# A decoder layer in one kernel: in its cross-attention GpSimd adds a bias one step sooner, and ScalarE copies scores ahead of two context pieces

## The reference

```python
x = x + _L0_attn_ref(_layernorm(x), ...)
x = x + _L0_xattn_ref(_layernorm(x), ctx_1024, ctx_1024, ...)
x = x + _L0_ffn_ref(_layernorm(x), ...)      # last: y = real(ifft(fft(x) @ w)) + bias

def _L0_xattn_ref(query, key, value, Wq, bq, Wk, bk, Wv, bv, Wo, bo):     # 16 heads of 32, TOPK 32
    q, k, v = heads(query @ Wq.T + bq), heads(key @ Wk.T + bk), heads(value @ Wv.T + bv)
    scores = einsum('bhqd,bhkd->bhqk', q, k) / SCALE
    top_scores, top_idx = top_k(scores, 32)
    w = softmax(top_scores)
    out = einsum('bhqk,bhqkd->bhqd', w, take(v, top_idx))
    return merge(out) @ Wo.T + bo
```

## Time and profile before

| | |
|---|---|
| median of 3 runs | 2591.87 us (2591.48 to 2596.62) |
| profiled execution, its own time | 2596.9 us |
| span of the profile | 2595.1 us |
| busy: TensorE, VectorE | 2147.9 us (83%), 1987.7 us (77%) |
| busy: ScalarE, GpSimd | 1272.3 us (49%), 1275.2 us (49%) |
| mean granted clock of TensorE | 0.915 of full |

### The profile page before, as it was taken

How to read it: one execution, slowest core, us unless ns; L and a number is a source line. 1 busy time by engine, 2 the same in 40 slices (tenths; PEclk the granted TensorE clock), 3 DMA queues, 4 the chain that set the end, 5 groups by cost and what they waited for, 6 DMA issues and landing times. The chain is left out here.

```text
span 2595.1 us, 54503 instructions
## 1 busy us (share of the span) xinstructions
PE 2147.9 (83%) x19760; PEld 1691.8 (65%) x19760; DVE 1987.7 (77%) x3663; ACT 1272.3 (49%) x2464; POOL 1275.2 (49%) x1473
## 2 busy tenths in 40 slices
PE   2787878787885479898899888898899889898976
PEld 1555555555562367777777777777777777777764
DVE  4666665657542169998988989889889898898995
ACT  3232323232320257666666566566566566656653
POOL 2464545545442145555555454555455455545543
PEclk9899999999987789999999898899899889989997
DMA  5000000000004300100000000000000010001000
GB/s 170 8 20 10 19 9 19 9 19 9 16 8 145 92 18 16 30 19 20 25 25 16 20 23 26 20 19 24 27 16 19 20 30 19 20 16 34 6 8 10
DMA packets 41511, 70.29 MB, mean 27 GB/s; under 512 B 4638, under 2 KB 21166, under 8 KB 41260
## 3 DMA queue, kind: packets, MB, share of 16 engines
q1 hardware_dynamic: 35868, 56.31, 7.1%
q0 software_dynamic: 3632, 7.58, 1.2%
q10 hardware_dynamic: 1760, 3.28, 0.5%
HBM read 60.54 MB, written 9.86 MB: 27 GB/s over the span
## 5 line engine op out<-in xcount | busy, mean ns | idle before, releaser
L1346 DVE MATCH_REPLACE8 ca_W<-ca_top,ca_W 128x722 f32<-128x722 f32 (+1 forms) x624 | 554.0, 896 | 0.0
L1334 DVE MAX8 ca_top<-ca_W 128x8 f32<-128x722 f32 (+1 forms) x624 | 537.8, 900 | 1.2
L949 POOL TENSOR_TENSOR ca_S<-ca_S,ca_W 128x722 f32<-128x722 f32 (+1 forms) x208 | 357.2, 1737 | 262.3 <-ACT ca_W L1208 262.3
L88 PE MATMUL ca_pS<-ca_KH,ca_QH 128*128 128x362 f32 (+1 forms) x384 | 156.3, 407 | 139.2 <-ACT ca_S L1225 131.7
L926 POOL TENSOR_TENSOR ca_KL<-ca_K,ca_KH 128x384 fp32r<-128x384 f32 (+1 forms) x128 | 114.3, 893 | 310.8 <-ACT ca_KH L1200 308.4
L1324 DVE MAX8 ca_top<-ca_S 128x8 f32<-128x722 f32 (+1 forms) x208 | 180.8, 902 | 111.1 <-ACT ca_S L1225 96.3
L1230 ACT ACTIVATE ca_PT<-ca_pT 128x768 f32<-128x768 f32 (+1 forms) x208 | 164.0, 788 | 182.4 <-PE ca_pT L1081 181.5
L88 PE MATMUL ca_pF<-ca_cH,ca_WkH 128*128 128x338 f32 (+1 forms) x512 | 199.0, 389 | 23.3 <-POOL ca_cL L934 23.3
L1114 PE MATMUL ca_pO<-ca_PT,ca_V 128*32 128x56 f32 (+5 forms) x4608 | 217.3, 225 | 0.0
L364 POOL TENSOR_TENSOR sa_ss<-sa_ss,sa_minus_half 100x16 f32<-100x16 f32 x64 | 191.1, 2994 | 22.3 <-DVE sa_ss L534 22.2
L1208 ACT ACTIVATE ca_W<-ca_W,ca_shift 128x722 f32<-128x722 f32 (+1 forms) x208 | 185.8, 893 | 22.8 <-DVE ca_W L1346 22.8
(11 more groups left out here) (213 smaller groups left out, 5231.7 us busy)
## 6 DMA issues: line engine op xcount, KB each, us to landing
ca_raw<-in_ctxT SPq DMA_DIRECT2D x32, 384.0 KB, 3.4
ca_raw<-in_ctxT SPq DMA_DIRECT2D x32, 338.0 KB, 3.1
sa_xin<-in_x SPq DMA_DIRECT2D x16, 200.0 KB
sa_xres<-in_x SPq DMA_DIRECT2D x16, 200.0 KB
x_scratch<-sa_x SPq DMA_DIRECT2D x16, 200.0 KB
x_scratch<-y_scratch POOLq DMA_DIRECT2D x16, 200.0 KB, 13.0
ca_xin<-x_scratch SPq DMA_DIRECT2D x16, 200.0 KB
ca_x<-x_scratch SPq DMA_DIRECT2D x16, 200.0 KB
```

The source lines that it names most:

```text
L88: pe.matmul(out, ah, bh, start=start, stop=False)
L949: pool.tensor_tensor(S[k][rows, :], S[k][rows, :], W[r][rows, :], ALU.subtract).then_inc(p_ready, 1)
L1334: n_of[t.i] = order.mark(dve.max(top[r][rows, 8 * k:8 * k + 8], W[r][rows, :]))
L1346: ins = dve.match_replace(W[r][rows, :], eight, W[r][rows, :], REMOVED)
```

## The change

Two moves, nothing is removed or added. On GpSimd the addition of `bias_f` goes from the end of step 5 into step 4, behind `context_low`. On ScalarE `context_high` of the pieces 1 and 3 (steps 1 and 4) goes behind the copy of the first scores, the first projections' copies and the first output copy.

```diff
@@ GpSimd, body @@
                     if s in (1, 4) and nxt:
                         context_low(bn, 2 * (s // 3) + 1)
+                    if s == 4 and prev:
+                        pool.wait_ge(xn2_ready, b.count(1, 0))
+                        pool.tensor_tensor(x2[:, :], x2[:, :], bias_f[:, :], ALU.add).then_inc(x2f_ready, 1)
                     if s == 5 and nxt:
                         query_low(bn)
...
-                    if s == 5 and prev:
-                        pool.wait_ge(xn2_ready, b.count(1, 0))
-                        pool.tensor_tensor(x2[:, :], x2[:, :], bias_f[:, :], ALU.add).then_inc(x2f_ready, 1)
@@ ScalarE, body @@
                     for x in last:
                         exps_left(*x)
-                    if s in (1, 4) and nxt:
-                        context_high(bn, 2 * (s // 3) + 1)
...
                     if coming:
                         keep_scores(*coming[0])
...
                     if old:
                         keep_output(*old[0])
+                    if s in (1, 4) and nxt:
+                        context_high(bn, 2 * (s // 3) + 1)
```

## The result

The change makes the kernel slower: 2612.8 us median (2612.15 to 2613.93, 4 runs) against 2594.22 (2591.48 to 2596.62, 4 runs), a ratio of 1.0072 with a 95% interval of 1.0055 to 1.0090. Forecast were 2595 us and 2585 to 2606: the time lies outside the range, on the side of rival (c). The profiled execution took 2613.15 us, its span is 2611.3, 16.2 more than before.

The account below looks back on a forecast made before the run. The loop was taken to run over TensorE, ScalarE, GpSimd and the context load, with VectorE's 6 us slack. Terms -1.25 + 4 + 0.5 = +3.2 us on the median 2591.87 gave 2595 us, no tellable change; range 2585 to 2606.

Parts of the forecast that it names:

- rival (c): Steps 1 and 4: half clock falls wholly on the projections; up to 13 + 14 us slower, 2600 to 2618; chance 0.31.
- Part 1: GpSimd's bias add moved into its step 4 pause: free there, VectorE's wait cut to 2.7 us, gain only in last batch.
- The term of -1.25 us: Earlier bias add: gained once, in the last batch, which VectorE paces; bounds 0 and 20 or even 53 us.
- Part 2: Step 1: score copy ahead of cH, projections start 0.5 us earlier, pause moves behind the scores; +4 us in all.
- the same 4.6 us of half clock counted from the restart: Step 1: mean half clock stays 4.6 us but counts from the projections, ending them +0.4 a batch, +6 us.
- The other case: Step 1: the clock comes back at the same instants as now, so the earlier projections gain 0.27 us a batch, -4 us.
- the term of +4 us: Step 1 over 15 batches: +6 us and -4 us weighed 4 to 1; bounds -25 and +13 us.
- always the long stretch, +0.9, +13 us: Step 1's upper bound: every batch has the long half-clock stretch, +0.9 us a batch, +13 us.
- The weight of one in five for unchanged instants: Step 1: share given to the clock returning at the same instants (-4 us), in weighing 4 to 1.
- Part 3: Step 4: scores earlier, projections start unchanged, half clock 4.6 us from restart; +0.1 a batch, taken as +0.5 us in all.
- the whole 6.5 us on the projections: Step 4's upper bound: all the half clock lies on the projections, +0.9 us a batch, +14 us.
- Rival (b): Clock stays up in step 1 or 4, as the scores break the pause; 25 or 29 us faster, near 2565; chance 0.10.

Follow-up runs that it names:

- bias: Only the GpSimd move of the bias_f add, applied to the kernel before: 2592.69 us, ratio 0.9989 (0.9977 to 1.0001).
- act4: Only ScalarE's context_high move in step 4, applied to the kernel before: 2592.16 us, ratio 0.9998 (0.9988 to 1.0009).
- act1: Only ScalarE's context_high move in step 1, applied to the kernel before: 2606.61 us, ratio 1.0048 (1.0031 to 1.0066).
- act14: Only the two ScalarE moves, in steps 1 and 4, applied to the kernel before: 2611.04 us, ratio 1.0060 (1.0043 to 1.0078).
- fill_act1: act1 plus 22 unused TensorE matmuls ahead of the wait for cL in step 1 only: 2557.40 us, ratio to before 0.9857.
- fill_after: The changed kernel plus unused TensorE matmuls ahead of the wait for cL, 22 in step 1, 17 in step 4: 2533.95 us, ratio to before 0.9762.
- fill_half: The changed kernel plus half the unused matmuls, 11 in step 1 and 8 in step 4: 2541.17 us, ratio to before 0.9789.

## Why the prediction was wrong

**What bounds the kernel: right.** VectorE's 6 us a batch were slack. `bias` freed 44 us of them in 13 batches, and the program gained 1 to 3 us, if anything.

**Part 1: right in each step.** The add stands in GpSimd's pause, which fell from 5.13 to 3.89 us (3.8 forecast); VectorE waits 2.7 us for the product; 2.2 us of new waits stand ahead of the first scores. The add takes 1.27 us beside VectorE's replacement and maximum, as the row had it, and the replacement beside it takes 0.90 us. The Trainium skill's page SBUF — State Buffer, "SBUF: two separate sides", has VectorE instructions with two SBUF inputs and those of GpSimd block each other; no such delay shows here. Whether the replacement counts as one with two inputs, no run here tells. Not foreseen was the wait for `rstd`, 13.3 us, which costs nothing, as VectorE does not pace. The term of -1.25 us measured -1.3 to -2.8 in `bias`, not clear of zero. In the last batch, where the prediction put it, ScalarE's waits for VectorE's replacements fell from 21.7 to 20.3 us.

**Part 2, the step that failed: half clock counted from the restart of the matmuls.** The order came as forecast: the copy ahead of `cH`, `cH` not later, the projections 0.45 us earlier (0.5 forecast), the pause 4.2 us (4.5). The term was built on "the same 4.6 us of half clock counted from the restart". Measured were 5.18 us in the mean. Counted so, 8 of 15 batches had a short stretch before (2.9 to 3.9 us), and only 2 have one now (3.0 us). At 0.45 us lost per microsecond the 0.58 us more are 0.26 of the 0.5 us a batch by which the term was short. The rest is in the other numbers of the sum: the projections ended 7.3 us behind the old start of the scores, not 7.4. (The 0.64 that the prediction puts behind the gap of 4.35 us belongs to another batch; the batch of that gap has 0.65.) The other case, a clock that comes back at the same instants, did not come either: it comes back 2.3 us later behind `cH`. So the term of +4 us, with its bound "always the long stretch, +0.9, +13 us", was at this bound: +0.89 a batch, 13.4 us. The weight of one in five for unchanged instants was wrong too: only in those 2 batches (8.68 and 8.80 us) is N below the old mean of 8.84.

**Part 3: the same step, and the larger miss.** The term was +0.5 us, the trace of the changed kernel has 0.74 a batch, 11.1 us. The start of the projections was right. But the half clock was again taken as 4.6 us from the restart of the projections, where 4.4 had been. In the traces the stretch keeps its 6.8 us, begins 1.5 us later, and lies with 5.7 us on the projections, where 4.3 did: close to the bound "the whole 6.5 us on the projections". That `act4` costs nothing agrees with the term of 0.5, but by luck, as a later stretch was shorter there. `act1` shows that a good half of the 0.74 (0.41) comes with the move in step 1. The prediction took the two places for independent, and they are not: with step 1's order changed, the stretch of step 4 begins 1.4 to 1.5 us later (`act1`, `act14`, the change), and with step 1 filled as well (`fill_act1`) it is back at its old place. The cause of this is open.

**The sum.** It had +3.2 us; the trace has 13.4 + 11.1 - 8.3 = 16.2. The 8.3 us that came back had no term. The 2.4 us of the tail among them are no doing of the bias add: the tail is as short in `act1` and `act4` (142.0 and 141.9 us), which lack that move. And the forecast started from 2591.87 us, where four runs of the kernel before have 2594.22, another 2.4 us.

**The chances.** Rival (c) had 0.31 and came true, in time and in mechanism: the row of projections takes the half clock which the scores and the pauses had absorbed. `fill_after` shows it: with the clock held up, N is no later in the order of the change than in that of before, in step 1 (7.54 against 7.73 and 7.49 us) and in step 4 (10.24 against 10.54 and 10.36), and nothing of the loss is left. Rival (b) did not come, as breaking the pause in two did not save the clock in step 4. The page TensorE: Matmul & The Clock Gate of the Trainium skill, section "HAM oscillation — how this bites in real kernels", states that each restart behind an idle gap is paid anew; the 79 us of `fill_after`, which fills two such gaps a batch, agree.

## What to carry to other kernels

Before an instruction is moved out of a pause of TensorE, ask what will run at half clock behind the pause: a short row of matmuls there can be cheaper than a long one, as the wait behind it hides a part of what it loses. A mean granted clock that stays the same (0.915 here) does not say that the clock costs the same: what counts is on which matmuls the half clock lies. Where a pause for a transfer returns in each iteration, unused matmuls in it, ending just before the data, can be worth more than any order: here 2.4% against a change of 0.7% the other way. And a wait of some 80 us in total, on an engine for which nobody waits, is worth next to nothing: 44 us freed, 1 to 3 gained.

## What the runs showed of the hardware

The half clock behind a pause of some 4 us lasted from 2.8 to 6.2 us on the matmuls, at the same places of different batches. It is not tied to their restart: it began in the pause, with the first matmul behind it, or up to 1.5 us later (`fill_half`). An unchanged place (step 4 in `act1`) got 0.9 us more of it through an edit elsewhere. Half of the filling, after which some 2 us of pause remain, kept the clock in 7 and 12 of 15 batches. And the matmuls on constants, 4.0 us for 22 of them, held it at full speed through a wait of 0.4 us and the 24 projections behind it.
